# A three-layer graph attention stack on one Trainium2 core: layers overlapped at their boundaries

## The reference

```
def gat_layer(x, src, dst, W, a_src, a_dst, b, n_nodes):
    h = x @ W
    s = h @ a_src
    d = h @ a_dst
    e = leaky_relu(s[src] + d[dst], 0.2)
    m = segment_max(e, dst)
    ex = exp(e - m[dst])
    z = segment_sum(ex, dst)
    return segment_sum((ex / z[dst])[:, None] * h[src], dst) + b
```

## Time and profile before

| | us |
|---|---|
| median of 3 runs | 814.06 (811.79 to 817.35) |
| profiled execution | 810.32 |
| its span, first to last instruction | 808.6 |
| VectorE busy | 720.8 (89%) |
| TensorE busy | 677.2 (84%), mean clock 0.918 |
| ScalarE busy | 524.4 (65%) |
| POOL busy | 299.4 (37%) |

### The profile page before, as it was taken

How to read it: one execution, slowest core, us unless ns; L and a number is a source line. 1 busy time by engine, 2 the same in 40 slices (tenths; PEclk the granted TensorE clock), 3 DMA queues, 4 the chain that set the end, 5 groups by cost and what they waited for, 6 DMA issues and landing times.

```text
span 808.6 us, 14270 instructions
## 1 busy us (share of the span) xinstructions
PE 677.2 (84%) x5705; PEld 657.9 (81%) x5705; DVE 720.8 (89%) x975; ACT 524.4 (65%) x826; POOL 299.4 (37%) x237
## 2 busy tenths in 40 slices
PE   4345988898978999999976989899993899898893
PEld 4345888898878999999975989899892899898893
DVE  5499999999959999999945999999993999999993
ACT  0053444434459987887835989788772998687680
POOL 1504000000014554544511546557461357474562
PEclk9996888788887999999996999999996799999997
DMA  3400000000000000000000000000000000110001
GB/s 98 109 0 1 1 2 1 1 1 1 2 0 18 17 1 17 17 2 1 1 4 17 1 17 16 2 17 1 1 1 3 17 17 2 32 32 2 17 3 34
DMA packets 11204, 10.63 MB, mean 13 GB/s; under 512 B 2258, under 2 KB 9295, under 8 KB 11120
## 3 DMA queue, kind: packets, MB, share of 16 engines
q1 hardware_dynamic: 10320, 8.27, 3.4%
q0 software_dynamic: 800, 1.26, 0.6%
HBM read 7.89 MB, written 1.64 MB: 12 GB/s over the span
## 4 chain that ended last, share of the span: by engine, by line
DVE 51%; PE 32%; issue 11%; DMA 2%; ACT 2%; POOL 1%; DVEq 0%; POOLq 0%; ACTq 0%
DVE ps L818 18%; PE ps L1401 17%; DVE scratch L656 14%; DVE scratch L946 10%; PE ps L1305 7%; DVE ps L821 3%; PE ps L1265 2%; PE ps L1457 1%; PE ps L1436 1%; DVE mu L834 1%; DMA edge_sb<-in_edges 1%; PE ps L1312 1%; DVE scratch L818 1%; PE ps L1410 1%; DMA gathered<-in_edges,start_i 1%
## 5 line engine op out<-in xcount | busy, mean ns | idle before, releaser
L507 POOL TENSOR_TENSOR scratch<-scratch 125x625 f32<-125x625 f32 x165 | 229.3, 1394 | 239.9 <-ACT scratch L1189 239.8
L1401 PE MATMUL ps<-hA,scratch 125*125 125x129 f32 x2300 | 272.8, 279 | 18.9 <-DVE scratch L946 16.5
L1401 PEld LDWEIGHTS ps<-hA,scratch 125*125 125x125 f32 x2300 | 265.0, 192 | 24.2 <-DVE scratch L946 21.5
L818 DVE SCALAR_TENSOR_TENSOR ps<-C,a_unit,ps 125x625 f32<-125x625 uint8 x330 | 278.9, 866 | 1.9
L946 DVE SCALAR_TENSOR_TENSOR scratch<-ps,r_src,C 125x625 f32<-125x625 f32 x210 | 180.7, 860 | 3.7 <-PE ps L1384 3.7
L1305 PE MATMUL ps<-scratch 128*128 128x125 bf16 x1250 | 148.4, 296 | 23.3 <-DVE scratch L656 17.1
L1305 PEld LDWEIGHTS ps<-scratch 128*128 128x128 bf16 x1250 | 143.1, 121 | 27.6 <-DVE scratch L656 21.1
L1184 ACT ACTIVATE scratch<-gathered,r_inv 125x625 f32<-125x625 f32 x165 | 133.2, 807 | 28.2 <-PE ps L1401 28.1
L1189 ACT ACTIVATE scratch<-scratch,r_src 125x625 f32<-125x625 f32 x165 | 147.8, 896 | 0.0
L1401 PE MATMUL ps<-hB,scratch 125*125 125x129 f32 x1150 | 136.4, 277 | 13.4 <-DVE scratch L946 11.3
L1401 PEld LDWEIGHTS ps<-hB,scratch 125*125 125x125 f32 x1150 | 131.0, 189 | 17.9 <-DVE scratch L946 15.1
(11 more groups left out here) (155 smaller groups left out, 493.6 us busy)
## 6 DMA issues: line engine op xcount, KB each, us to landing
gathered<-g_lines SPq DMA_DIRECT2D x12, 305.2 KB
xr<-in_x SPq DMA_DIRECT2D x1, 1562.5 KB
out<-xr SPq DMA_DIRECT2D x5, 312.5 KB
edge_sb<-in_edges SPq DMA_DIRECT2D x1, 805.7 KB
w<-in_W SPq DMA_DIRECT2D x2, 128.0 KB
gathered<-in_edges,start_i POOLq DMA_INDIRECT x5, 6.2
w<-in_W SPq DMA_DIRECT2D x1, 64.0 KB
av<-in_a_src SPq DMA_DIRECT2D x4, 0.5 KB
```

What stands on the lines that cost most here:

```text
L507: g.tensor_tensor(A, A, wide[n % 2], ALU.mult).then_inc(pool_done[L], 1)
L818: v.scalar_tensor_tensor(dest, counts, a_unit[:, s:s + 1], top, ALU.min, ALU.max).then_inc(top_done[L], 1)
L1401: last = mm(ps[0:P, acc_at(t):acc_at(t) + HW], A[:, P * t:P * (t + 1)], feat, start=opens and t in (0, 3), stop=closes, skip_group_check=True)
```

## The change

Chunks are now numbered through the layers, q = 0 to 14, and all tables, semaphores and loops run over q, so that the first chunk of a layer (`turn(q)`) is worked on while the last chunk of the layer before is dealt with, by tables of its own (TURN). Nothing branches inside the layers. In parts:

- The scale of the next layer is set from the extremes of its first 15 tiles (EARLY_TILES), in step 1 of the last chunk, widened to both sides by half of their width for layers 1 and 2. The extremes of the last ten tiles are taken in step 19 of the turn. In step 2 of the next chunk VectorE compares them with the guess (`set_mode`). If a guess failed, or the width is over the limit, everything is computed again at the end, in the careful way; each engine reads that flag once, after its last chunk.
- Extremes over partitions go through memory: a store of 125 pairs, a wait, a load of all 250 numbers to every partition and a reduction on VectorE (`exchange`, `over_nodes`), in place of POOL's reduction. POOL forms the scalars.
- Every layer's features are written to hA, and POOL scales them into hB for layers 1 and 2, five tiles at a time (`scale_tiles`), with the column of ones among the 645 elements of a partition. ScalarE scales only in layer 0, from hA to hB.
- `g_row` is stored from [125 partitions, tiles] straight to memory, transposed by the access pattern (`write_lines`); the transpose into `g_lines` and its copy are gone.
- Maxima no longer use the exact width as scale but the constant limit.
- In the last chunk of layers 0 and 1 the steps of the chain stand up to two earlier (BEFORE_LAST). In a turn the tops of tiles 20 to 24 stand at steps 21 to 23 and the row passes for steps 21 and 23 at steps 20 and 21.
- The last chunk's result is formed by VectorE in one operation a tile (`last_result`); POOL has added the bias to x before.
- r_src, e_src, g_row, a_unit and the other vectors of a layer have two buffers.

The diff, cut to its core; the pieces of chunk functions are those of POOL, VectorE and ScalarE in this order:

```
+        At = namedtuple("At", "tops chain kappa z stats pool pe act rest_pe rest_act")
+        USUAL = (At(1, (3, 4, 5, 6), 6, (8, 9, 10), None, (14,), (12, 15, 21), (14, 17, 23), 18, 20),
+                 At(1, (3, 4, 5, 6), 6, (8, 9, 10), (13, 14), (14, 19), (18, None, 21), (16, 20, 23), None, None),
+                 At(1, (3, 4, 5, 6), 6, (8, 9, 10), None, (14, 17, 20), (None,) * 3, (None,) * 3, None, None))
+        BEFORE_LAST = (At(1, (3, 4, 5, 6), 6, (8, 9, 10), None, (14,), (12, 14, 19), (13, 16, 21), 17, 18),
+                       At(1, (3, 4, 5, 6), 6, (8, 9, 10), (13, 14), (14, 19), (17, None, 19), (16, 19, 21), None, None))
+        TURN = (At(None, (1, 1, 2, 2), 3, (3, 3, 3), None, (11,), (7, 9, 13), (9, 12, 15), 11, 13),
+                At(None, (1, 1, 2, 2), 3, (3, 3, 3), (8, 8), (11, 15), (14, None, 16), (13, 14, 17), None, None))
+        EXPS = {(0, 0): 1, (1, 0): 2, (1, EARLY_TILES): 3, (1, LATE): 4, (2, 0): 5, (2, EARLY_TILES): 6, (2, LATE): 7}
...
+        def top_at(q, k):
+            if turn(q) and k >= LATE:
+                return (21, 21, 22, 22, 23)[k - LATE]
             return (k - AHEAD) * (T - 3) // (T - 1 - AHEAD)
...
+        def pass_at(q, s):
+            if turn(q) and s >= LATE:
+                return q * T + 20 + (s - LATE) // 2
+            return q * T + s - PASS_AHEAD
...
+            def write_lines(L, t0, t1):
+                sp.wait_ge(g_done, LINES[L, t0])
+                sp.dma_start(g_d[L, t0 * P:t1 * P].rearrange("(t p) -> p t", p=P), g_row[L % 2][:, t0:t1],
+                             allow_slow_non_contiguous=True).then_inc(lines_stored, 16)
...
+            def exchange(e):
+                sp.wait_ge(ext_ready, e + 1)
+                sp.dma_start(ext_d[e, :].rearrange("(p i) -> p i", i=2), ext[:, :]).then_inc(ext_out, 16)
+                sp.wait_ge(ext_out, 16 * (e + 1))
+                sp.dma_start(ext_rows, ext_d[e, :].unsqueeze(0).broadcast_to([P, 2 * P])).then_inc(ext_in, 16)
+
+            exchange(0)
+            write_lines(0, 0, T)
...
-                g.partition_all_reduce(extg[:, :], ext[:, :], P, MAX_OVER_PARTITIONS).then_inc(extg_ready, 1)
...
+            def scalars(L):
+                most, least = extg[L % 2][:, 0:1], extg[L % 2][:, 1:2]
+                high, low = wide_ext[L % 2][:, 0:1], wide_ext[L % 2][:, 1:2]
+                width, margin = spread[L % 2][:, 0:1], spread[L % 2][:, 1:2]
+                n = 5 * L
+                pool.wait_ge(extg_ready, L + 1)
+                g.tensor_tensor(width, most, least, ALU.add).then_inc(scal_lin, 1)
+                g.tensor_scalar(sigma[L % 2][:, :], most, least, (1.0 - SLOPE) / 2, ALU.subtract,
+                                ALU.mult).then_inc(scal_lin, 1)
+                pool.wait_ge(scal_lin, n + 1)
+                g.tensor_scalar(margin, width, 0.5 if L else 0.0, None, ALU.mult).then_inc(scal_lin, 1)
+                pool.wait_ge(scal_lin, n + 3)
+                g.tensor_scalar(wide_ext[L % 2][:, :], extg[L % 2][:, :], margin, None, ALU.add).then_inc(scal_lin, 1)
...
+            def scale_tiles(L, t0):
+                t1 = t0 + CT
+                pool.wait_ge(exps_ready, EXPS[L, 0 if t0 < EARLY_TILES else t0])
+                pool.wait_ge(F.pe_done, (L * NC - 1) * T + t1)
+                g.tensor_tensor(hB3[:, t0:t1, :], hA[:, t0:t1, :],
+                                e_src[L % 2][:, t0:t1].unsqueeze(2).broadcast_to([P, CT, HW]),
+                                ALU.mult).then_inc(y_scaled, 1)
+
+            def last_bias():
+                xc = xr[:, (NC - 1) * CT:T, :]
+                pool.wait_ge(F.g_ready, NC)
+                g.tensor_tensor(xc, xc, b3r[:, :].unsqueeze(1).broadcast_to([P, CT, D]), ALU.add).then_inc(b3_added, 1)
...
+                    if c == NC - 1 and L < LAYERS - 1:
+                        if s == 11:
+                            scalars(L + 1)
+                            pool.wait_ge(scal_lin, 5 * (L + 2))
+                            cuts(L + 1, 0, EARLY_TILES)
+                            units(L + 1, 0, EARLY_TILES)
+                            backs(L + 1, 0, EARLY_TILES, 2 * L + 1)
+                        if s in (17, 21, 23):
+                            scale_tiles(L + 1, (17, 21, 23).index(s) * CT)
+                    if turn(q):
+                        if s == 3:
+                            pool.wait_ge(F.new_sb, q - 1)
+                            units(L, EARLY_TILES, LATE)
+                        if s == 5:
+                            scale_tiles(L, EARLY_TILES)
+                        if s == 21:
+                            pool.wait_ge(F.new_sb, q)
+                            cuts(L, EARLY_TILES, T)
+                            units(L, LATE, T)
+                            backs(L, EARLY_TILES, T, 2 * L)
+                            scale_tiles(L, LATE)
+                    if q == Q - 1 and s == 22:
+                        last_bias()
+                    if s in POOL_S:
+                        block_product(q, s)
...
+            def extremes_late(L):
+                dve.wait_ge(F.new_sb, L * NC)
+                dve.wait_ge(ext_out, 16 * 2 * L)
+                extremes(L, EARLY_TILES, T)
+                dve.wait_ge(ext_lin, EXT_NO[L] + 1)
+                v.tensor_reduce(ext[:, 1:2], a_neg[:, EARLY_TILES:T], AX.X, ALU.max).then_inc(ext_ready, 1)
+
+            def over_nodes(e, into, done):
+                dve.wait_ge(ext_in, 16 * (e + 1))
+                v.tensor_reduce(into[:, :], ext_rows.rearrange("p (n i) -> p i n", i=2), AX.X, ALU.max).then_inc(done, 1)
...
+            def set_mode(L):
+                width, ok = spread[L % 2][:, 0:1], within[:, 0:1]
+                if L:
+                    dve.wait_ge(all_ready, L)
+                    for i in range(2):
+                        dve.wait_ge(within_lin, 3 * L - 2 + i)
+                        v.tensor_scalar(ok, ext_all[:, i:i + 1], wide_ext[L % 2][:, i:i + 1], ok, ALU.is_le,
+                                        ALU.mult).then_inc(within_lin, 1)
+                    dve.wait_ge(within_lin, 3 * L)
+                    v.tensor_scalar(ok, width, SPAN_LIMIT / 2, ok, ALU.is_le, ALU.mult).then_inc(within_lin, 1)
+                else:
+                    dve.wait_ge(sig_ready, 1)
+                    v.tensor_scalar(ok, width, SPAN_LIMIT, covers[:, :], ALU.is_le, ALU.mult).then_inc(within_lin, 1)
+                if L == LAYERS - 1:
...
+                    if c == NC - 1 and L < LAYERS - 1:
+                        if s == 1:
+                            extremes_early(L + 1)
+                        if s == 6:
+                            over_nodes(2 * L + 1, extg[(L + 1) % 2], extg_ready)
+                        if s == 12:
+                            inverse_r(L + 1, 0, EARLY_TILES)
+                    if turn(q):
+                        if s == 5:
+                            inverse_r(L, EARLY_TILES, LATE)
+                        if s == 19:
+                            extremes_late(L)
+                        if s == LATE:
+                            inverse_r(L, LATE, T)
+                    if L and c == 1 and s == 2:
+                        over_nodes(2 * L, ext_all, all_ready)
+                        set_mode(L)
+                if q < Q - 1:
+                    for k in range(AHEAD):
...
+            def last_result():
+                q = Q - 1
+                for part in range(4):
+                    fast_maxima(q, part)
+                dve.wait_ge(kappa_ready, Q)
+                for part in range(3):
+                    sums_inverse(F, q, part)
+                dve.wait_ge(F.rz_ready, Q)
+                dve.wait_ge(b3_added, 1)
+                for t in range(CT):
+                    xt = xr[:, (NC - 1) * CT + t, :]
+                    last = v.scalar_tensor_tensor(xt, raw[:, t, 0:D], rz[:, t:t + 1], xt, ALU.mult, ALU.add)
+                dve.wait_ge(y_ready, NC - 1)
+                last.then_inc(y_ready, 1)
...
-            def scale_features(L, s):
-                a_.activation(h_of[L][:, s, 0:D], h_of[L][:, s, 0:D], ACT.Copy,
-                              scale=e_src[:, s:s + 1]).then_inc(h_scaled[L], 1)
+            def scale_features(s):
+                a_.activation(hB3[:, s, :], hA[:, s, :], ACT.Copy, scale=e_src[0][:, s:s + 1]).then_inc(h_scaled, 1)
...
+                    if c == NC - 1 and L < LAYERS - 1:
+                        if s == 10:
+                            act.wait_ge(sig_ready, L + 2)
+                            exps_dst(L + 1, 0, EARLY_TILES)
+                            exps_src(L + 1, 0, EARLY_TILES)
+                        if s == T - 1:
+                            act.wait_ge(F.new_sb, q)
+                            exps_src(L + 1, EARLY_TILES, LATE)
+                    if turn(q):
+                        if s == post_at(q).act[2]:
+                            act.wait_ge(F.new_sb, q)
+                            exps_src(L, LATE, T)
+                        if s == 22:
```

(5 more changed lines are left out.)

1549 lines of the change are left out of this document (790 added, 759 removed).

## The result

The changed kernel takes 786.65 us (median of 4 runs, 785.29 to 787.33); the kernel before, timed on the same chip, 812.92 (4 runs). The ratio is 0.967, with a 95% interval of 0.962 to 0.971: faster. Timed again later it took 786.70, at 0.969 [0.967, 0.971]. The forecast was 783.6, in a range of 773 to 802. The profiled execution took 787.33 with a span of 785.6, 23.0 less than the span before of 808.6; my sum had 30.5 less. That is luck.

The account below looks back on a forecast made before the run. TensorE bounds layer 0, VectorE layers 1 and 2, with some 20 us a turn lacking bulk work. Terms -1.0 + 1.5 - 17.9 + 1.7 + 3.2 - 17.7 + 2.7 - 3.0 = -30.5: 783.6 us from the median, range 773 to 802.

Parts of the forecast that it names:

- The turns: Each layer's turn overlaps the last chunk: stretches of 54.84 and 55.91 us become 36.9 and 38.2, -17.9 and -17.7.
- Chunk 4 of layer 1: Last chunk of layer 1: 1.2 us of extremes and reciprocal, 0.5 for the row, 1.5 for delayed x: +3.2 us.
- POOL's burst delays the x: Chunk 4 of layer 1: POOL's scalars delay the x that VectorE's statistics wait for, 1.5 us (0 to 3).
- Start: Before layer 0's chunks: extremes exchanged through memory in 4.5 us without loss, mode branch gone: -1.0 us (0 to -1.2).
- Layer 2: Second chunk of layer 2: VectorE reads late extremes and judges the guess, its lead gone: +2.7 us; later chunks no term.
- Scaling: Layers 1 and 2: feature scalings move from ScalarE into POOL's idle time: 0, up to 2 us a turn if features late.
- Row lines: Chunk 4: 1875 four-byte numbers stored singly, 9.8 us, 15.2 with wait and load, inside 16.4: 0.
- Tail: Last chunk's end: five VectorE operations replace three POOL passes, bias already in: -3.0 us (-2 to -3.5).
- A: Rival: everything lands in its slot, the waits of both turns and POOL's 2.5 us vanish: 776 us; chance 0.20.
- B: Rival: the chain comes late in the turns (43 and 45 us) and the clock falls: 799 us; chance 0.20.
- C: Rival: slow four-byte stores delay ScalarE's first pass of a new layer; at 113 ns a number 837 us; chance 0.05.
- D: Rival: the guess fails and the careful layers run after all, far over the time of before; chance 0.01.

Follow-up runs that it names:

- two kernels: On the changed kernel with the start's new order and constant products: POOL's scalars at step 13, 781.66 us; that plus POOL's first scaling at step 19, 781.41 us.

## Why the prediction was right or wrong

In brackets stand my terms, then what was measured.

*The turns* (-17.9 and -17.7; -19.4 and -20.0). Right in mechanism, in the wait and in the clock. The step that was off in the first is the 1.7 us for TensorE's rest of the hidden layer: TensorE wrote it at 439.37, right behind its own products, without a wait.

*Chunk 4 of layer 1* (+3.2; +6.2) and its turn are one account. Predicted the pair was 36.9 + 38.2 = 75.1, and it is 75.8 (75.3 when timed again). The split was wrong, because the cut follows TensorE's last products, and TensorE stood 1.7 us for ScalarE's normalised tiles and 4.7 in all for VectorE's products while VectorE worked on: of its 0.86 us operations for the maxima it worked on 28 in chunk 4 and on 22 in the turn, where each chunk has 25 to do. The pair is mostly VectorE's: 70.3 us of work, and 3.1 of waiting for the late features' copies, in every one of these runs. TensorE's waits in chunk 4 could be moved away (two kernels) and the pair fell by only 0.6. What I called the step "POOL's burst delays the x" was there, and was small: VectorE waited 0.9 us for it and not 1.5, and the 0.6 came in the two kernels where this wait is gone.

*Start* (-1.0; +2.5). The step that failed is "beside half a one-hot on VectorE, and no loss". I priced the exchange's latency, too low at 4.5 for 7.3, and didn't ask what is queued behind the two instructions that wait for it. Put behind their neighbours they cost nothing; that run also shows that 7.3 us of exchange are not the loss. The reduction on POOL in its place, 8.9 us to POOL's next instruction, gave no start outside the scatter either.

*Layer 2* (+2.7 and 0; +3.8 and +2.5). The chunks behind the second had no term in my sum, since nothing in them changed, and the granted clock was no part of it. It was at 1.00 in the first two of the three before, at 0.95 in the last, and is at 0.95 in all three now. With TensorE kept busy through its wait these three take 100.0 us, as before (99.9), and not the 102.4 of the changed kernel. The wait itself was there before too, 2.1 us, with the clock at 1.00 behind it; what tips it now is not shown. The 1.1 us too much in the second chunk are not the clock's. There VectorE's short operation e_top starts at 647.11 beside a product of POOL (646.97 to 648.26) and takes 1.17 us for 0.15. In the four runs with the exchange and a clock of 0.95 in this chunk e_top meets none, and the chunk takes 34.3 to 34.5, where I had 34.2; at 1.00 e_top or its neighbour m_top does, and it takes 35.1 to 35.3. In the two runs in which VectorE came to it with a lead of two operations it is 33.9. So the lower clock cost the three chunks behind and not this one: what it costs goes by where VectorE's short operations fall.

*Scaling* (0): right in the choice, 1.8 us cheaper than ScalarE; the 0 itself is not shown. *Row lines* (store 9.8, inside 16.4 with the rest): hidden, as forecast, with a price of 6.96 us, or 18.6 ns for each of my 375 numbers of a queue, all of it counted, where I took 26. The slack was mis-sized the other way: from the store's issue to the pass at 595.67 are 15.5 us where I had 21.1, so 4.4 are left of it. *Tail* (-3.0; -2.2, and 2.6 by the experiment): right in mechanism, 0.4 to 0.8 too much.

*Rivals.* A (776) needed all waits gone and they are not. B is out: no clock under 1.00 in a turn of the changed kernel. The clock fell where neither B nor I had looked. C's mechanism is real, shown by making the stores three times as many, which takes 20 of the 25 us; at the true price it is far off. D didn't happen, as the time without careful layers shows.

## What to carry to other kernels

Price a moved step also by its alternative: a reduction that seems to take 0.4 us can block its engine's queue for 7 to 15, and that shows only once something stands behind it; look at what an engine does after such an instruction, not at its duration. Price a wait by what is queued behind it on the same engine, and move it behind its neighbours when the answer can arrive meanwhile. And don't judge a moved step by one stretch: three of these edits shortened a chunk by 1 to 2 us and lengthened the next, and only the pair showed that VectorE's work and its one long wait made up most of the two. Where an engine is the bound and its chunks still differ by a microsecond at equal work, look at its shortest operations: here one of 0.15 us took up to 1.17 beside another engine's long one.

## What the runs showed of the hardware

- POOL's partition reduction: 0.37 us busy (2.03 the first time), then 6.91 to 8.54 us until the next POOL instruction in all five, and twice 5.95 and 6.37 us ahead of it, all with no wait shown. Why is not settled.
- Small POOL operations beside a bf16 one-hot of VectorE took 1.37 and 1.53 us and ended with it; alone they took 0.19 and 0.33. The same the other way round: operations of VectorE on 125x5 elements that started beside a float32 product of POOL ended 0.02 us behind it and took up to 1.17 us, for 0.15 alone. Which resource they share is not shown.
- Writing 250 numbers to memory and spreading them over the partitions took 7.3 us beside running work, 3.1 of it from the store's issue to the load's.
- A store of 1875 separate four-byte numbers was 1880 packets and took 6.8 to 7.0 us, and a second and third in a row 7.0 each.
- TensorE idle for some 2.2 us was followed by passes at the lower clock in some chunks and not in others of equal work; kept busy with a constant it never was.
